# Four-row hybrid block: the first group of row 0 tile by tile through four banks, row 2's fourth expert stage behind row 3's attention, and casts, masks and side steps at other places

## What is computed

```
def _L0_attn_a_ref(x, Wq, Wk, Wv, lambda_params, g1, g2, g3, W1, W2):
    xn = _rms(x, g1)
    ...
    pQ = jax.nn.elu(Q); pK = jax.nn.elu(K)
    ...
    kv1 = jnp.einsum('bshe,bshd->bsed', K1, V) * SCALE
    w1 = jnp.einsum('bshe,bsed->bshd', Q1, kv1)
    ...
    attn = w1 - lmb * w2
    attn = (1.0 - LAMBDA_INIT) * _rms(attn, g2)
    attn = _rms(attn, g3) + attn
    h = jax.nn.gelu(jnp.einsum('bse,fe->bsf', attn, W1), approximate=False)
    return jnp.einsum('bsf,ef->bse', h, W2) + attn

def _L0_attn_b_ref(x, w_qkv, w_out, b_out):
    ...
    allowed = (j <= i) & (i - j < WINDOW)
    attn = jax.nn.softmax(scores, axis=-1)
    ...

def _L0_ffn_ref(hidden_states, gate_w, gate_up_w, down_w):
    probs = jax.nn.softmax(x @ gate_w.T, axis=-1)
    top_w, top_idx = jax.lax.top_k(probs, 8)
    ...
    def body(acc, ws):
        guw, dw, w_e = ws
        g, u = jnp.split(x @ guw.T, 2, axis=-1)
        return (acc + (u * silu(g)) @ dw.T * w_e[:, None], None)

x = x + _L0_attn_a_ref(_layernorm(x), ...)
x = x + _L0_ffn_ref(_layernorm(x), ...)
x = x + _L0_attn_b_ref(_layernorm(x), ...)
x = x + _L0_ffn_ref(_layernorm(x), ...)
```

## Time and profile before

| | |
|---|---|
| median of three runs | 1049.34 us (1046.89 to 1050.1) |
| the profiled execution | 1050.18 us |
| its span in the trace | 1048.4 us |
| mean granted clock of TensorE | 0.959 of full speed |
| TensorE, PEld | 89%, 62% of the span |
| VectorE, ScalarE, GpSimd | 62%, 58%, 63% |

### The profile page before, as it was taken

One profiled execution on the slowest core, in us unless ns is written; L12 is line 12 of the kernel. 1 busy time (PEld: TensorE's weight loads), 2 busy tenths in 40 slices (PEclk: granted clock), 3 DMA queues, 4 the chain that ended last, 5 costly groups with the idle time before them and its releaser, 6 DMA issues.

```text
span 1048.4 us, 16649 instructions
## 1 busy us (share of the span) xinstructions
PE 938.2 (89%) x5472; PEld 649.0 (62%) x5472; DVE 646.9 (62%) x1444; ACT 609.1 (58%) x1865; POOL 657.5 (63%) x607
## 2 busy tenths in 40 slices
PE   3246999889999999999999998999999999988998
PEld 1034665568666666668666665668666666676665
DVE  5884785447775864779737854779744343576432
ACT  4246565657366557689384566689364453875432
POOL 5763778444568874857668764857655645454654
PEclk9998999866899999999999999999999999988999
DMA  5004343101435543541234433541153555011652
GB/s 176 1 0 94 80 91 73 41 2 42 103 85 119 110 104 83 121 95 43 61 83 107 106 81 84 121 94 43 41 122 82 123 122 124 19 42 28 137 123 60
DMA packets 63224, 85.67 MB, mean 82 GB/s; under 512 B 3681, under 2 KB 29090, under 8 KB 62882
## 3 DMA queue, kind: packets, MB, share of 16 engines
q1 hardware_dynamic: 63138, 84.61, 35.8%
HBM read 79.32 MB, written 5.28 MB: 81 GB/s over the span
## 4 chain that ended last, share of the span: by engine, by line
PE 63%; ACT 12%; DVE 6%; POOL 6%; issue 5%; DMA 1%; DVEq 0%; SPq 0%; ACTq 0%; POOLq 0%
PE bank L1378 17%; PE bank L1353 8%; PE bank L1355 8%; PE bank L1354 8%; ACT probs L953 4%; PE bank L1414 4%; PE bank L1399 4%; PE bank L1428 2%; POOL work L776 2%; PE bank L1392 1%; PE bank L1251 1%; PE bank L1257 1%; ACT work L933 1%; ACT L933 1%; DVE probsT L1199 1%
## 5 line engine op out<-in xcount | busy, mean ns | idle before, releaser
L776 POOL TENSOR_TENSOR work<-work,spread_w 128x512 f32<-128x512 f32 x256 | 336.8, 1327 | 186.0 <-DVE work L1158 164.9
L1158 DVE TENSOR_TENSOR work<-work,bank 128x512 f32<-128x512 f32 x256 | 174.4, 682 | 242.4 <-ACT work L933 144.3
L1378 PE MATMUL bank<-work,down_w 128*128 128x512 f32 x512 | 265.3, 602 | 10.1 <-ACT yT L945 5.6
L933 ACT ACTIVATE work<-bank 128x512 f32<-128x512 f32 x256 | 150.8, 595 | 179.4 <-PE bank L1355 175.9
L953 ACT ACTIVATE probs<-bank,neg_max 128x96 f32<-128x96 f32 x512 | 165.7, 381 | 32.5 <-DVE neg_max L1185 19.9
L1353 PE MATMUL bank<-z_hi,gate_hi 128*128 128x512 f32 x256 | 171.9, 671 | 0.0
L784 POOL TENSOR_TENSOR probs<-probs,prob_inv 128x768 f32<-128x768 f32 x64 | 94.0, 1469 | 89.5 <-DVE prob_inv L1193 89.4
L953 ACT ACTIVATION_READ_ACCUMULATOR probs<-bank,neg_max 128x1 f32 x512 | 125.2, 248 | 0.0
L1378 PEld LDWEIGHTS bank<-work,down_w 128*128 128x128 f32 x512 | 95.8, 191 | 39.8 <-POOL work L776 11.3
L1355 PE MATMUL bank<-z_hi,gate_lo 128*128 128x512 f32 x256 | 102.6, 401 | 0.0
L1353 PE MATMUL bank<-z_hi,up_hi 128*128 128x512 f32 x256 | 102.2, 399 | 0.0
(11 more groups left out here) (142 smaller groups left out, 1467.3 us busy)
## 6 DMA issues: line engine op xcount, KB each, us to landing
spread_w<-comb_dram SPq DMA_DIRECT2D x128, 512.0 KB, 6.7
vals<-v_dram SPq DMA_DIRECT2D x16, 384.0 KB, 4.2
x_buf<-x SPq DMA_DIRECT2D x8, 256.0 KB, 3.3
v_dram<-v_tok SPq DMA_DIRECT2D x8, 256.0 KB, 6.7
out<-xs SPq DMA_DIRECT2D x8, 256.0 KB, 5.1
spread_w<-wg SPq DMA_DIRECT2D x1, 1024.0 KB, 6.4
spread_w<-wu SPq DMA_DIRECT2D x1, 1024.0 KB, 8.5
comb_dram<-combT SPq DMA_DIRECT2D x16, 64.0 KB, 1.6
```

The costliest lines, as they stand in the source:

```text
L776: pool.tensor_tensor(work[:, n % WORK], work[:, n % WORK], spread_w[:, n // EACH % 2, s % EACH], ALU.mult).then_inc(hid_gated, 1)
L933: act.activation(work[:, n % WORK], bank[GATE_BANKS[ring_of(row, f, s)]], ACT.Silu).then_inc(silu_ready, 1)
L1158: dve.tensor_tensor(work[:, n % WORK], work[:, n % WORK], bank[UP_BANKS[ring_of(row, f, s)]], ALU.mult).then_inc(gated_ready, 1)
L1378: pe.matmul(bank[Y_BANK], down_w[:, c], work[:, n % WORK], start=(c == 0), stop=(c == CH - 1)).then_inc(down_done, 1)
```

## The change

Six things are changed.

1. **First group.** `qkv`, `expo`, `elu` and `qscale` of row 0's group 0 are replaced by `qkv_first`, `elu_first` and a tilewise `qscale_first`: the products of the four tiles go to banks 0 to 3, and copy, relu, exponential and elu are done for each tile. The weights of `qkv` get a semaphore of their own and are loaded ahead of the second half of x. TensorE waits for the router's weights only at `route`, for the MLP's at `mlp1`.
2. **Casts.** In `AHEAD` the cast of the up weights and its difference (`w_hi` 1, `w_lo` 1) stand behind `h_gain` and `mlp1` of group 0, and that of the gate weights' difference behind `wred` 3.
3. **Masks.** The other three head groups of the window mask (`masks` 2) stand in period 0's `third`, behind the weighting of slot 3. The memset moves into `masks` 1, and the DMA of the 64 zero values moves into `first_values`.
4. **Periods 3 and 4.** Period 3 has `first`, `second`, `third` (48 chunks) and the attention; period 4 has `fourth` of row 2, then `second` and `last` of row 3 (48 chunks). The steps of group 1's norm, keys, queries and values stand inside row 3's attention, and the router chain that stood there goes behind it.
5. **Row 3's sum** is written into `x_buf` (`sum_of`), without the wait for `x_stored`.
6. **Side steps** in `PLAN`, (0, first), (0, third), (0, attn), (1, third) and (1, fourth) are moved by some slots.

The core of the diff:

```diff
 def stages_of(period):
     if period < ROWS:
         yield "first", period, 0
-    if period:
-        yield "second", period - 1, G
-    if period < ROWS:
+        if period:
+            yield "second", period - 1, G
         yield "third", period, 1
-    if period:
-        yield "fourth", period - 1, G + 1
-    if period < ROWS:
+        if 0 < period < ROWS - 1:
+            yield "fourth", period - 1, G + 1
         yield "attn", period, None
+    else:
+        yield "fourth", ROWS - 2, G + 1
+        yield "second", ROWS - 1, G
+        yield "last", ROWS - 1, G + 1
...
     (0, "third"): {
...
-        2: ahead(("expo", 1), ("elu", 1)),
-        3: ahead(("h_scale", 0), ("qscale", 1), ("attend", 4)),
+        3: ahead(("expo", 1), ("elu", 1), ("h_scale", 0), ("masks", 2)),
+        4: ahead(("qscale", 1), ("attend", 4), ("h_sq2", 0)),
...
     (0, "attn"): {
-        1: ahead(("m_apply", 0)),
...
+        11: own(("values", 1)) + ahead(("m_apply", 0)),
...
     (ROWS - 1, "attn"): {
-        8: back(("y_back", 3)),
-        17: own(("proj", 0), ("m_stats", 2), ("m_rstd", 2)),
...
+        3: own(("y_back", 1), ("s_stats", 1), ("s_rstd", 1)),
+        4: own(("s_apply", 1)),
+        6: own(("seq_turn", 1)),
+        7: own(("keys", 1)),
+        8: own(("queries", 1)),
+        11: own(("values", 1)),
+        26: own(("proj", 0)),
...
+        def sum_of(row):
+            return xs if row < ROWS - 1 else x_of(row)
...
             load_rows(0, 0)
+            for dst, src in qkv_a_loads:
+                sp.dma_start(dst, src).then_inc(qkv_a_loaded, 16)
             load_rows(0, 1)
...
-                late = period in (0, ROWS - 1)
+                late = period == 0
...
-                    if period:
+                    if 0 < period < ROWS - 1:
                         store_half(row - 1, 1)
...
             def mask_rest():
-                pool.wait_ge(kv_terms_ready, T)
+                pool.wait_ge(hid_gated, chunk(0, 1, MASK_SLOT) + 1)
...
             def attend(row, i):
-                pool.wait_ge(elu_ready, group(row, i // T) + 1)
+                if row == 0 and i < T - 1:
+                    pool.wait_ge(elu_first, i + 1)
+                else:
+                    pool.wait_ge(elu_ready, group(row, i // T) + 1)
...
+            def qkv_first(row, i):
+                act.wait_ge(qkv_first_ready, i + 1)
+                act.activation(qkv[:, i], bank[i][:, 0:3 * D], ACT.Copy)
+                act.activation(elu[:, i], bank[i][:, 0:2 * D], ACT.Relu, scale=-1.0).then_inc(relu_ready, 1)
+                act.wait_ge(relu_ready, i + 1)
+                act.activation(elu[:, i], elu[:, i], ACT.Exp, scale=-1.0)\
+                   .then_inc(exp_first if i < T - 1 else exp_ready, 1)
...
             def proj(row, g):
-                wait(dve, x_stored[g], 16 * row)
-                add_side(xs, x_of(row), g, row, "proj", g, attn_b_done, group(row, g) + 1)
+                if row < ROWS - 1:
+                    wait(dve, x_stored[g], 16 * row)
+                add_side(sum_of(row), x_of(row), g, row, "proj", g, attn_b_done, group(row, g) + 1)
...
+            def qkv_first(row, i):
+                if i == 0:
+                    pe.wait_ge(qkv_w_ready, 1)
+                    pe.wait_ge(side_taken, SIDE_AT[0, "x_turn", 0] + 1)
+                pe.matmul(bank[i][:, 0:3 * D], zT[:, P * i:P * (i + 1)], qkv_a_w[:],
+                          start=True, stop=True).then_inc(qkv_first_ready, 1)
...
             pe.wait_ge(ident_ready, 1)
-            pe.wait_ge(attn_a_loaded, 16 * len(attn_a_loads))
-            pe.wait_ge(qkv_w_ready, 1)
-            pe.wait_ge(router_ready, 1)
             run_ahead(steps)
```

More of the change, by code:

```diff
@@ L128 @@
[L128 to L136 removed]
+        3: ahead(("x_apply", 1), ("h_newton1", 0)),
@@ new lines @@
+        4: ahead(("h_newton2", 0), ("h_rg", 0)),
+        5: back(("y_back", 2), ("m_apply", 3)) + ahead(("x_turn", 1), ("h_scale", 0)),
+        6: ahead(("h_sq2", 0)),
+        7: back(("moe_turn", 3), ("z_hi", 3)) + ahead(("h_red2", 0), ("h_pow2", 0)),
+        8: back(("z_lo", 3)) + ahead(("h_gain", 0)),
+        9: back(("route", 3), ("r_sum", 3)) + ahead(("h_sum", 0), ("x_add", 0)),
+        10: back(("top", 3)) + ahead(("qkv", 4)),
+        11: back(("weigh", 3)) + ahead(("attnT", 0)),
+        12: back(("comb", 3)) + ahead(("qkv", 5)),
```

230 lines of the change are left out of this document (130 added, 100 removed).

## The result

The changed kernel is slower, by 1.0% to 1.4%. Its median is 1063.11 us (four runs, 1059.81 to 1073.79), the kernel before takes 1049.72 us (four runs, 1046.89 to 1052.47), and the ratio is 1.014 with a 95% interval of 1.0073 to 1.0206. Forecast was 1044.5, with a range of 1032 to 1057. Measured again beside the experiments, over six runs, the changed kernel takes 1061.67 us, ratio 1.0099 (1.0065 to 1.0133), which by the ratio is 10.4 us more than the kernel before.

What follows compares the result with a forecast made beforehand. TensorE bounds period 3's chunks; attentions lose time to waits and half clock. Terms -5.5, -1.5, 0, +6.5, -0.7, -1.5, -2.0 sum to -4.7 from 1050.2: 1045.5, put at 1044.5 against the median; range 1032 to 1057.

Steps and rivals of the forecast that it cites:

- The start: Row 0's first group tile by tile: an 8 us lead is lost again in VectorE's queue; 0, from -8 to +3.
- the up cast alone: In the start, the moved cast beside small GpSimd instructions costs at most 1.23 us more; 4.9 beside a long one.
- The masks: Ten GpSimd instructions moved into row 0's second stage delay later weightings and make TensorE stand: +6.5 us, from +2 to +9.
- the copy's slot: Cast `expo 1` one slot later lets ScalarE's copy of the finished sum go before its table load: -0.7 us.
- row 0's attention: `m_apply` goes from hook 1 to hook 11, where TensorE at half clock covers it: -1.5 us, from -8 to +8.
- periods 1 and 2: The 2.20 us wait of the turn for VectorE becomes 1.30 with the new slots: -2.0 us, from -4 to +2.
- Row 3's attention and the change of sides: Attention 69 us against 74.5, waits for spread and `proj` gone: -5.5; matmuls exchanged with the TensorE-bound stretch: -1.5.
- the half clock: In row 3's attention, one stretch of 9 us or a little more at half clock, costing about 5 us.
- the 63.7 that I had as base: Row 3's attention before any half clock: row 1's 57.2 us plus 5.9 of ScalarE work and 0.6 of waiting.
- The 1.5 us for the matmuls that change sides: Group 1's keys, queries and values leave the TensorE-bound stretch, router chain and `proj` enter: -1.5 us, from -3 to 0.
- Rival D: Slower, 1061 us: row 3's attention falls into the pattern of row 0's, 86 us in place of 69; chance 0.11.

Runs made afterwards that it cites:

- e4: The kernel before with parts 1 and 2 alone (the new start), the masks in the first 40 us: 1055.96 us, ratio 1.0050.
- e7: e4 with the difference gate_lo computed on VectorE behind the gate weights' cast, in place of GpSimd: 1051.84 us, ratio 1.0004.
- e6: The kernel before with part 3 alone, the masks behind slot 3 of row 0's second stage: 1059.43 us, ratio 1.0079.
- e2: The changed kernel with the ten mask instructions back in the first 40 us on GpSimd: 1056.37 us, ratio 1.0048.
- e3: The kernel before with parts 4 and 5 alone: 1049.28 us, ratio 0.9968.
- e10: e9 with part 6's edits of row 0's attention alone: 1043.05 us, ratio 0.9954.
- e9: e7 with parts 4 and 5 added, masks and side steps as in the kernel before: 1050.18 us, ratio 0.9988.
- e13: e10 measured again, no edit: 1043.26 us, ratio 0.9936.
- e8: The changed kernel with weighT back from slot 15 to slot 13 of the fourth stages: 1058.03 us, ratio 1.0075.
- e14: e13 with part 6's new slots of period 0's two stages added, masks still early: 1046.26 us, ratio 0.9976.
- e12: The changed kernel with masks early, gate_lo on VectorE and weighT at slot 13: 1049.60 us, ratio 1.0003.

## Why the prediction was wrong

The forecast's sum was -4.7 and the changed kernel is at +10.4. Part 6 makes about 7 us of these 15, the start 5, and row 3's attention with the change of sides 4; the masks came out 1 below their term.

**The start** (forecast 0, ends -8 and +3; measured +3 in both profiles, +5.3 by e4's ratio). The lead of 8 us, its loss to VectorE's queue and the shorter wait for the squares came as worked out. The step that failed is the sentence in which the up cast alone was moved beside GpSimd. The diff moves `w_lo` 0 as well, 4.5 us of GpSimd, from beside a VectorE with nothing urgent to do to beside the head sums on which the first weighting waits. VectorE loses 4.0 us there (5.27 less 1.23), and e7 gives back 4.1 in the median. The Trainium skill (SBUF — State Buffer, "Who interferes with whom") says that a VectorE instruction with two inputs in SBUF contends with a GpSimd instruction that reads SBUF. That whoever issues first has the shared ports for its whole instruction it says of VectorE's two-port modes. The trace agrees with the first and shows the second for this instruction of two inputs as well: issued 0.31 us behind gate_lo, it ended 1.08 us behind it. I had applied the rule to the instruction that I was following, not to every instruction that changed its neighbour.

**The masks** (+6.5; measured 5.3 in the changed kernel, 8.3 by the ratio of e6). Right in place and mechanism, and in size within the uncertainty: a stand of 4.83 us at the down matmul, with half clock behind it. The block of 8.46 us from which I worked was 6.9 us long at the new place, which is one reason for the smaller figure.

**Part 6** (-4.2 for the copy's slot, row 0's attention and periods 1 and 2; measured about +3 in the changed kernel, by difference: e2's 5.0 less e4's 5.3 plus e3's 3.4, uncertain by some 4 us, and 10.3 alone). This is the largest error, as the +3 is a net of gains and losses. *Row 0's attention* gained, and more than the 1.5: with the new hooks it takes 82.5 to 85.4 us in ten profiles, without them 82.9 to 93.2 in seven, with a mean 4 us higher, and e10 gains 7.1 on e9 (by the ratios 3.6, with overlapping intervals; e13 is 5.5 below e9 by them). That TensorE covers `m_apply` there is not what parts the profiles: they differ in the time at half clock, 27 to 41 us with the new hooks and 31 to 61 without, and two kernels without them (e4, e7) are as quick as those with them. Why the long stretches stay away stays open. *Periods 1 and 2* had the wrong sign in period 1 (+3.8 and +3.9 in the profiles of the changed kernel) and no clear effect in period 2 (176.2 to 178.2 us with the new slots, 176.0 to 177.7 with the old): I read the new slots as the pattern of the period with the shorter wait, and they are the other one: the wait at the turn is 2.42 us in period 1 and 2.33 in period 2 of the profile after. *weighT* I had passed over; its late place costs 2.5 to 3.6 by e8, which is inside the uncertainty, and the two waits of TensorE in front of each attention that it makes are sure. Here a step with a TensorE product and a ScalarE copy that moved to the last slot in front of an attention came to stand in front of that attention's table load. *Period 0's slots* cost 3 us in the median of e14 and 3.2 to 4.9 in its profile, where I had -0.7 for one of them; the step is the wait of `seq_turn` for ScalarE.

**Row 3's attention and the change of sides** (-7.0; measured -3.4 by e3). The wait for the spread and the wait for `proj` went as forecast. With the new order it takes 71.0 to 74.4 us in twelve profiles; with the old one, 74.3 to 81.0 in five. The term that was mis-sized is the half clock: I had counted one such stretch and there are two, 20 us in all. If all of that time is TensorE's work, it makes 10 of the 73.3 and leaves the 63.7 that I had as base; this is worked out and not shown. The 1.5 us for the matmuls that change sides came to nothing: 230.4 us for the 96 chunks in place of 230.7.

That the masks, gate_lo and `weighT` together carry the loss is shown by e12, which undoes all three and is back at the kernel before; the share of each is known to a few us only. What is not settled is how the parts share their costs: alone, parts 3 and 6 cost 8.3 and 10.3 us, beside the others 5.3 and about 3. Stretches at half clock that come in either case would do that; it wasn't tried.

**Rival D** named the slower side but the wrong place: in the new order row 3's attention never passed 74.4, so that 1061 was met is chance. The masks stayed inside their bounds and the start at its upper one in the profiles, above it by e4's ratio. What took the sum past the range beside that is what had a narrow bound or none: periods 1 and 2 (at most +2), period 0's slots and `weighT`.

## What to carry to other kernels

When a diff moves a step, list for each engine which instruction now runs beside it, and price both neighbours; an instruction that was harmless beside idle or early work can stop a critical one for its whole length, as gate_lo did. A short wait for an in-order engine tells what may not be moved in front of it, so look which steps the new slot puts ahead of the releasing instruction. And a step that ends in a small copy should not be the last before a table load that a whole phase waits for.

The fastest kernel here is e10 and e13: tilewise start, gate_lo on VectorE, row 2's fourth stage behind row 3's attention, and the new hooks in row 0's attention, with masks and all other slots as before. It takes 1043.2 us, 0.5% to 0.6% below the kernel before.

## What was not expected of the hardware

The granted clock that a window shows has to be read with the length of the matmuls at the program's start. After, the window from 20 to 74 us has 0.50 and before it has 1.00, TensorE being busy for a third of either (after, then before):

```profile
20.00:74.00 54.00, 18.61 (x44) 9.96 (x44) 44.02 (x65) 17.81 (x39) 28.96 (x16) 0.50 0.00 0
```

```profile
20.00:74.00 54.00, 15.77 (x35) 7.00 (x34) 43.06 (x62) 17.13 (x36) 37.66 (x30) 1.00 0.00 0
```

But the two matmuls of a tile's product take 1.65 us in both (timelines, after, then before), and before they take 0.91 only at 90.20. The same `z_hi,up_lo` matmul takes 0.63 us at 85.90 and 0.39 at 88.31:

```profile
28.59 1.65 PE L1318 MATMUL bank<-qkv_a_w,zT 128*128 128x384 f32 x2 [0.69 <-ACT zT L860]
```

```profile
79.60 1.65 PE L1257 MATMUL bank<-qkv_a_w,zT 128*128 128x384 f32 x2 [0.69 <-ACT zT L825]
...
85.90 0.63 PE L1355 MATMUL bank<-z_hi,up_lo 128*128 128x512 f32 x1
...
88.31 0.39 PE L1355 MATMUL bank<-z_hi,up_lo 128*128 128x512 f32 x1
...
90.20 0.91 PE L1257 MATMUL bank<-qkv_a_w,zT 128*128 128x384 f32 x2 [0.85 <-ACT elu L846]
```

The trace's record of the clock has its first entry at 86.69 us before and at 15.54 after, each time a rise to full speed, and time ahead of the first entry is shown as 1.00. By the lengths of the matmuls it was half speed: TensorE ran slowly for the first 86 us before, and the 1.00 of the earlier trace rows is not a measurement. In all kernels with the old start the first entry lies at 77 to 87 us, in all with the new one at 14 to 17.

So the mean clock of the execution (0.91 to 0.93 with the new start, 0.95 to 0.96 without) can't be compared between the two starts: e13, the fastest, has 0.932. If the time ahead of the first entry is counted as half speed, the kernel before has about 0.92 by my estimate and e13 about the same.
